# A graph kernel's edge stage: ScalarE's relu halves and seeds ahead of the message's upper parts, VectorE's attribute remainder behind the one-hot

## What is computed

```python
def layer0(x, src, dst, edge_attr, W1, b1, W2, b2, Wg, bg, gamma, beta):
    ei = concatenate([x[src], edge_attr], axis=-1)
    core = maximum(ei @ W1 + b1, 0.0) @ W2 + b2
    gate = sigmoid(ei @ Wg + bg)
    agg = segment_sum(gate * core, dst, num_segments=N)
    return layernorm(agg + x) * gamma + beta
x = layernorm(x + layer0(...))
x = layernorm(x + layer1(x, ...))   # two hops of a normalised sum over edges, then a linear map and log_softmax
```

## Time and profile before

| | |
|---|---|
| median of 3 runs | 2568.09 us (2565.17 to 2568.68) |
| span of the profiled execution (it has no other time of its own) | 2722.1 us |
| PE busy over the span | 2389.6 us, 88% |
| DVE busy | 2076.2 us, 76% |
| ACT busy | 1493.1 us, 55% |
| POOL busy | 1663.0 us, 61% |

### The profile page before, as it was taken

One profiled execution on the slowest core, in us unless ns is written; L12 is line 12 of the kernel. 1 busy time (PEld: TensorE's weight loads), 2 busy tenths in 40 slices (PEclk: granted clock), 3 DMA queues, 4 the chain that ended last, 5 costly groups with the idle time before them and its releaser, 6 DMA issues.

```text
span 2722.1 us, 50965 instructions
## 1 busy us (share of the span) xinstructions
PE 2389.6 (88%) x16049; PEld 1845.0 (68%) x16049; DVE 2076.2 (76%) x4860; ACT 1493.1 (55%) x2727; POOL 1663.0 (61%) x1581
## 2 busy tenths in 40 slices
PE   7879999999999999999899894689888899888864
PEld 3479999999999998888889881245444444444443
DVE  6658888888889888888889998897777763436455
ACT  1157777777767776676767674454665640112123
POOL 0367777777677776667667661456555645666663
PEclk9989999999999999999999996899999999998976
DMA  6555555555555555555555542254455425665542
GB/s 210 207 154 158 161 167 160 161 163 164 157 160 164 165 157 161 164 170 169 164 163 165 161 143 83 80 138 126 119 142 140 126 92 189 209 228 162 188 129 88
DMA packets 276289, 422.45 MB, mean 155 GB/s; under 512 B 127634, under 2 KB 198692, under 8 KB 274004
## 3 DMA queue, kind: packets, MB, share of 16 engines
q0 software_dynamic: 90368, 281.11, 34.6%
q1 hardware_dynamic: 170028, 116.99, 14.3%
q10 hardware_dynamic: 15656, 21.30, 2.3%
HBM read 354.91 MB, written 64.37 MB: 154 GB/s over the span
## 4 chain that ended last, share of the span: by engine, by line
PE 53%; DVE 18%; issue 9%; ACT 8%; another core or an unknown queue 7%; DMA 2%; DVEq 1%; POOL 1%; ACTq 1%; SPq 0%; POOLq 0%
PE banks L972 15%; PE banks L1060 5%; PE banks L949 5%; PE banks L1034 4%; PE banks L1086 3%; PE banks L856 3%; ACT counts L1432 2%; PE banks L1102 2%; PE banks L946 2%; DVE hidden_lo L1767 2%; PE banks L947 2%; ACT hidden_hi L1296 2%; DVE room L1786 2%; PE banks L960 2%
## 5 line engine op out<-in xcount | busy, mean ns | idle before, releaser
L797 POOL DMA_INDIRECT gathered<-p_table,src_t x784 | 807.2, 1030 | 439.7 <-DVE gate L1778 252.8
L797 POOL DMA_INDIRECT gathered<-hop_table,src_t x576 | 585.5, 1017 | 463.1 <-PE banks L1102 174.8
L972 PE MATMUL banks<-w_hi,hidden_hi 128*128 128x256 f32 x1568 | 462.1, 295 | 55.1 <-DVE hidden_lo L1767 48.6
L972 PE MATMUL banks<-w_lo,hidden_hi 128*128 128x256 f32 x1568 | 443.6, 283 | 0.0
L972 PE MATMUL banks<-w_hi,hidden_lo 128*128 128x256 f32 x1568 | 443.5, 283 | 0.0
L1432 ACT CAST counts<-banks 128x686 f32 (+3 forms) x382 | 295.4, 773 | 213.8 <-PE banks L1037 103.8
L1303 ACT CAST msg_hi<-room 128x512 fp32r<-128x512 f32 x392 | 241.8, 617 | 246.4 <-DVE room L1786 209.5
L1767 DVE SCALAR_TENSOR_TENSOR hidden_lo<-banks,hidden_hi 128x512 fp32r<-128x512 f32 x392 | 270.1, 690 | 121.8 <-ACT hidden_hi L1296 68.4
L972 PEld LDWEIGHTS banks<-w_hi,hidden_hi 128*128 128x128 f32 x1568 | 299.6, 191 | 79.0 <-DVE hidden_lo L1767 66.5
L1034 PE MATMUL banks<-codes,low_hot 128*128 128x343 f16 (+3 forms) x958 | 242.2, 337 | 111.2 <-DVE codes L2002 54.6
L1317 ACT ACTIVATE gate<-gate 128x512 f32<-128x512 f32 x392 | 242.3, 632 | 123.0 <-DVE gate L1778 107.1
(11 more groups left out here) (225 smaller groups left out, 5280.3 us busy)
## 6 DMA issues: line engine op xcount, KB each, us to landing
ea<-in_edge_attr SPq DMA_DIRECT2D x196, 128.0 KB
counts_saved<-counts SPq DMA_DIRECT2D x16, 1568.0 KB
ring<-counts_saved SPq DMA_DIRECT2D x16, 1568.0 KB
gathered<-p_table,src_t POOLq DMA_INDIRECT x784
p_table<-p_t ACTq DMA_DIRECT2D x48, 256.0 KB, 4.1
hop_table<-parts SPq DMA_DIRECT2D x12, 896.0 KB
gathered<-hop_table,src_t POOLq DMA_INDIRECT x576
x_saved<-x_room SPq DMA_DIRECT2D x7, 896.0 KB
```

Of the source, the lines that this page charges most:

```text
L797: pool.indirect_dma_start(out=rows[:, n % slots, j, :], out_offset=None, in_=table[:, :], in_offset=bass.IndirectOffsetOnAxis(ap=src_t[:, ...
L972: last = nc.tensor.matmul(banks[:, 4 + half, j % 2 * H:(j % 2 + 1) * H], lhs, rhs, start=False, stop=n == len(products) - 1, skip_group_ch ...
```

## The change

Two orders inside a step change, both in the edge stage. ScalarE runs both relu halves and the seeds of group g+1 first, and the two upper parts of the message of group g behind them. VectorE runs lower_ea behind message and one_hot, and the second place of node work with it. Nothing is added or removed, and no semaphore changes.

```diff
@@ ScalarE, step(i, s)
                 at_group(round_ea, i, s, 4)
                 if in_order and isinstance(i, int):
                     node_rows_at(2 * i + s)
-                at_group(upper_msg(0), i, s, 0)
                 at_group(upper_hidden(0), i, s, 1)
-                at_group(upper_msg(1), i, s, 0)
                 at_group(upper_hidden(1), i, s, 1)
                 at_group(seed_core, i, s, 1)
+                at_group(upper_msg(0), i, s, 0)
+                at_group(upper_msg(1), i, s, 0)
                 at_group(open_gate, i, s, 1)
@@ VectorE, step_in_order(i, s)
                 at_group(add_window, i, s, -2)
                 at_group(lower_msg, i, s, -1)
                 node_work_at(0)
-                at_group(lower_ea, i, s, 4)
-                node_work_at(1)
                 at_group(message, i, s, 0)
                 at_group(one_hot, i, s, 0)
+                node_work_at(1)
+                at_group(lower_ea, i, s, 4)
                 node_work_at(2)
                 at_group(lower_hidden(0), i, s, 1)
                 at_group(lower_hidden(1), i, s, 1)
```

## The result

| kernel | median | ratio to before, same set of runs [95%] |
|---|---|---|
| before, 7 runs | 2565.58 us (2564.61 to 2568.68) | |
| changed, 7 runs | 2573.43 us (2566.52 to 2577.24) | 1.0023 [1.0012, 1.0034] |
| changed, second set | 2578.46 us | 1.0039 [1.0025, 1.0054] |
| changed, third set | 2578.78 us | 1.0044 [1.003, 1.0059] |

One thing has to be known to read the numbers: the kernel before takes 2566 to 2568 us in the median in four sets of runs (the shorter kind) and 2694 and 2729 us in two others (the longer kind), so each kernel is compared within its own set. The profile shown ahead of the prediction (span 2722.1) is of the longer kind; the profile of before that I use from here on is a new one with a span of 2560.1 (c0). The changed kernel's profile has a span of 2572.4, 12.3 us more.

The account below looks back on a forecast made before the run. The prediction took TensorE to bound the edge stage. Its terms, -12 - 2 - 6 + 5 + 3 = -12 us, took the timed median from 2568.1 to 2556 us (chance 0.48), range 2536 to 2580.

Parts of the forecast that it names:

- the one on the gathers: GpSimd's queue: lower_msg waits for the later upper part, so gathers start 0.6 us later; +5 us, bounds 0 and 24.
- The first stretch: Edge stage before 745 us: relu mostly waits for TensorE in either order, so almost nothing gained; 2 us, bounds 0 and 5.
- Part 1: ScalarE: relu halves and seeds before the upper parts let hidden_lo start earlier; -12 us after 745 us, -2 before.
- Part 2: VectorE: the attribute remainder behind the one-hot loses its wait for ScalarE's rounding; -6 us, bounds 0 and 18.5.
- The port: VectorE's and GpSimd's lower_msg can collide on the shared SBUF port; +3 us, bounds 0 and 15.
- B: GpSimd's queue, lower_msg before the gathers: late gathers decide and it gets slower, +12 us, 2580 us; chance 0.16.
- A: TensorE's late semaphore to relu takes the gain back; change worth 0 to 5 us, 2565 us; chance 0.18.
- C: Relu halves free VectorE in all late steps with little given back; -30 us, 2538 us; chance 0.10.
- D: Groups 78 to 165: VectorE's lower_msg waits for GpSimd's at the port, +15 us, net +3, 2571 us; chance 0.08.
- the idle before L946 grows by more than 10 us: TensorE's wait before the hidden product, which also needs gathered rows: this growth would show the forecast wrong.

Follow-up runs that it names:

- e6: Kernel before, with GpSimd's lower_msg also waiting for the first half of add_gate, in the set of 2694 us: 1.0011.
- e9: Kernel before, with GpSimd's lower_msg also waiting for the first half of add_gate, in a set of the shorter kind: 1.0137.
- e8: Kernel before, with ScalarE's order both relu halves, first upper part, seeds, second upper part, in a set of the shorter kind: 0.9968.
- e13: Kernel before, with only the second place of node work moved behind the one-hot on VectorE: 0.999.
- e14: Kernel before, with only lower_ea moved behind the one-hot on VectorE, node work left, against a set of 2728.7 us: 1.0069.
- e15: Kernel before, with SyncE's attribute load held until ScalarE's second relu half, against a set of 2728.7 us: 0.9983.
- e11: Changed kernel, but with the first upper part ahead of the seeds on ScalarE, in a set of the shorter kind: 0.9972.
- e12: Kernel before, with only ScalarE's second upper part moved, behind the seeds: 0.9961, 2556.9 us.
- e4: Kernel before, with ScalarE's order both relu halves, first upper part, seeds, second upper part, in the set of 2694 us: 1.0153.
- e5: Changed kernel, but with the first upper part ahead of the seeds on ScalarE, in the set of 2694 us: 1.0144.
- e3: Changed kernel, but with GpSimd's lower_msg between the second and third gather: 1.022, 2622.83 us.

## Why the prediction was wrong

- **The step that failed is the one on the gathers: "Bounds: 0, and 0.6 us in some 40 groups, 24 us. I take 5."** The delay was read rightly (0.6 foreseen, 0.68 measured), and so was nearly the number of steps that pay (43 waits at L946, 34 more than before). The price was +28.5 us of waits, above the upper bound: 0.84 us for each added wait, and more with TensorE's busy time. "The landing has slack in most steps" was true and didn't help. In half of the recorded groups L946 starts more than 0.5 us behind the last landing, and the loss comes from the other ones. The sum took 5 from a span of 0 to 24 with no reading of how many landings are near.
- **The first stretch had no term for a loss.** The prediction reasoned that before 745 us there is nothing to win. In a run of the shorter kind TensorE never idles from 180 to 700 us, so no order could win there and whatever holds TensorE is lost: 17.8 us. The profile that was read, of the longer kind, hid this, with 14 us of idle time in it. e6 and e9, one kernel in either kind of set, cost 0.1% and 1.4%; why they differ stays open.
- **Part 1, -12 and -2: right in kind, and in size somewhat low.** L972's wait fell by 18.2 us, 15.2 with ScalarE's part alone. The upper ends were 18.7 and 5. Not all of the 18.2 need be the relu's order: e8, with both relu halves first and the gathers on time, has only 7.2 of them, and a TensorE that is late at L946 waits less at L972. How they divide wasn't measured.
- **Part 2, -6: wrong in sign.** Alone it costs 10.9 us of steps. The prediction named the next wait, "the core product's second half", and still booked a gain. Work in front of a wait that comes anyway is free, and the remainder had been standing there: its wait of 32.5 us went, and one of 32.5 came before the message. This explains why nothing is won. What then costs is seen at L946 (+11.7 us), not at L972 (-4.7), and the cause isn't shown: it takes the remainder's move (e13, e14), by e14 and e15 more than the load's, and with ScalarE's order of e8 it costs no time that can be told (e11).
- **The port, +3: the collision came, without a price on the path.** VectorE's lower_msg went from 680 to 757 ns (after 700 us) while GpSimd's stayed at 1208. That is 120 x 0.077 = 9 us of VectorE time. The mean before 700 us is 782 ns. In the steps there VectorE then waits for the core product (0.62 us before the message's second half), so it is hidden. After 700 us no run takes the collision away by itself: e8 takes it away (681 ns) together with the late gathers. By the rule of the Trainium skill cited in the prediction ("SBUF — State Buffer", "Who interferes with whom") a VectorE instruction that meets a running GpSimd one would wait to its end. In the step of 484.46 GpSimd's runs from 484.63 to 485.84 and VectorE's starts at 485.62: 0.22 us of overlap, and VectorE's takes 0.76 us, 0.08 more than alone, less than the rule says (GpSimd's ends are rough). The prediction's own row was read too kindly: what was left of the one-hot when lower_msg started was 0.46 us (1064.67 - 1064.21), and lower_msg got 0.3 longer.
- **The rivals.** B is what happened, in its place and by its mechanism, with part 2's loss added. Its +12 us is near the +7.9, +10.5 and +10.5 us of the three sets. Its "point from which it decides", 35 groups, was met with 43 waits. That the total comes so near is luck in part: B has part 2 as a gain. A asked that the late signal of TensorE eat the gain; in the sets of the shorter kind that signal isn't late (in the step of 484.46 the transposes end at 488.47 and the relu starts at 488.51). C and D did not come.
- **The signs named in advance** worked: "the idle before L946 grows by more than 10 us" is what the trace shows (+28.5).

What stays open: why the signal is late in some sets, and what decides it (the chip numbered 4 ran a set of either kind, so the chip alone doesn't); what the changed kernel and e12 do in a set of the longer kind, where e4 and e5 lost 1.5% though they win in the other; and by what way VectorE's part lengthens the wait at L946.

## What to carry to other kernels

When an instruction moves, follow it through the queues of the other engines too: look for what waits for it, what stands behind the waiter in the same queue, and how long the cover of that was. Ask of each wait that goes what work it was hiding, and what work stands ahead of the next wait. And compare the span of a profile with the timed runs before reading slack from it: here it was 6% longer, and showed idle time in the first stretch that a run of the shorter kind doesn't have.

## What the runs showed of the hardware

- The same program took 2566 to 2568 us in four sets of runs and 2694 and 2729 in two. In steps of the longer kind ScalarE's relu starts 1.4 us and 2.1 us (e4) after the recorded end of the transposes that it reads, and 0.04 us after it in the changed kernel's step. The mean step of groups 4 to 77 was 7.35 us against 7.01 in the two profiles of before, with the granted clock at 1.00 in both stretches. The same order of ScalarE's work (e4, e8) gave +1.5% in one and -0.3% in the other.
- Four gathers in GpSimd's queue are a chain of about 0.95 us each with 0.30 us between them. A delay of 0.6 us at their start cost 35 us over 196 groups in a set of the shorter kind (e9) and nothing that can be told in one of the longer (e6); 1.2 us inside the chain cost 2.2% (e3).
- A wait of TensorE took more than its recorded idle: in the step of 491.47 0.84 us for 0.61 of idle.
